# Local attention: the exp of each head taken by ScalarE from PSUM, with the negated maximum as bias and the total as accumulator output

## What is computed

```
sim  = einsum('bhwie,bhwje->bhwij', bq, bk2) * QK_SCALE
sim  = where(mask, -max, sim)
attn = softmax(sim, -1)
out  = einsum('bhwij,bhwje->bhwie', attn, bv2)
```

## Time and profile before

| | us |
|---|---|
| median of 3 runs | 4217.94 |
| lowest and highest | 4217.25, 4219.12 |
| the profiled execution | 4230.46 |
| its span, first to last instruction | 4228.0 |

### The profile page before, as it was taken

How to read it: one execution, slowest core, us unless ns; L and a number is a source line. 1 busy time by engine, 2 the same in 40 slices (tenths; PEclk the granted TensorE clock), 3 DMA queues, 4 the chain that set the end, 5 groups by cost and what they waited for, 6 DMA issues and landing times. The chain is left out here.

```text
span 4228.0 us, 154817 instructions
## 1 busy us (share of the span) xinstructions
PE 3986.5 (94%) x61339; PEld 2359.9 (56%) x61339; DVE 3368.7 (80%) x5724; ACT 2583.2 (61%) x5027; POOL 2537.1 (60%) x2772
## 2 busy tenths in 40 slices
PE   5888697999999999999999999999999999999998
PEld 3555486555554555545555545555455555455554
DVE  5777455899976999958999769999489997699994
ACT  4776222566665666665666656666666666566665
POOL 2111133777763777727777537777277775477771
PEclk8999998999999999999999999999999999999999
DMA  2000000000000000000000000000000000000001
GB/s 72 0 0 1 0 0 3 3 0 0 0 21 7 0 0 0 0 21 6 0 0 0 21 6 0 0 0 0 21 6 0 0 0 21 6 0 0 0 0 41
DMA packets 12340, 27.26 MB, mean 6 GB/s; under 512 B 2460, under 2 KB 6728, under 8 KB 11344
## 3 DMA queue, kind: packets, MB, share of 16 engines
q1 hardware_dynamic: 12240, 25.72, 1.7%
HBM read 23.62 MB, written 2.10 MB: 6 GB/s over the span
## 5 line engine op out<-in xcount | busy, mean ns | idle before, releaser
L954 POOL TENSOR_TENSOR w_t<-w_t 128x512 f32<-128x512 f32 x768 | 981.2, 1278 | 509.0 <-DVE w_t L1259 508.8
L1259 DVE TENSOR_TENSOR w_t<-banks,w_tab 128x512 f32<-128x512 f32 x1536 | 981.6, 681 | 46.1 <-PE banks L1130 27.7
L989 POOL TENSOR_TENSOR w_t<-w_t,w_rn 128x512 f32<-128x512 f32 x768 | 784.9, 1043 | 243.1 <-ACT w_rn L1434 243.1
L1069 PE MATMUL banks<-w_vo,w_xs 128*32 128x256 f32 x12288 | 823.2, 385 | 8.6 <-ACT w_us L1382 8.6
L1130 PE MATMUL banks<-w_qk,w_xs 128*128 128x512 f32 x1536 | 767.2, 622 | 5.8 <-issue 4.1
L1069 PEld LDWEIGHTS banks<-w_vo,w_xs 128*32 128x32 f32 x12288 | 321.7, 109 | 499.8 <-issue 368.6
L1393 ACT ACTIVATE w_pr<-w_pr 128x512 f32<-128x512 f32 x384 | 242.0, 630 | 581.8 <-DVE w_pr L1306 581.8
L1382 ACT ACTIVATE w_us<-banks 128x512 f32<-128x512 f32 x768 | 457.3, 596 | 173.1 <-PE banks L1069 173.1
L1288 DVE TENSOR_REDUCE w_ss<-w_sq 128x16 f32<-128x1024 f32 x384 | 464.3, 1209 | 0.0
L1108 PE MATMUL banks<-w_us,w_prT 128*32 128x128 f32 x10752 | 418.3, 276 | 20.7 <-issue 9.4
L981 POOL TENSOR_TENSOR w_pr<-w_pr,w_rl 128x512 f32<-128x512 f32 x384 | 403.1, 1050 | 35.0 <-DVE w_rl L1274 35.0
(11 more groups left out here) (176 smaller groups left out, 5838.2 us busy)
## 6 DMA issues: line engine op xcount, KB each, us to landing
w_qk<-w_qk_in SPq DMA_DIRECT2D x7, 1024.0 KB, 4.8
w_v<-w_v_in SPq DMA_DIRECT2D x7, 512.0 KB, 5.5
w_o<-w_o_in SPq DMA_DIRECT2D x7, 512.0 KB, 6.3
m_w<-m_w_in SPq DMA_DIRECT2D x6, 342.0 KB
xT<-x_in SPq DMA_DIRECT2D x4, 512.0 KB
out<-kept SPq DMA_DIRECT2D x8, 256.0 KB, 2.4
m_w<-m_w_in SPq DMA_DIRECT2D x6, 171.0 KB
r_tab<-r_tab_in SPq DMA_DIRECT2D x1, 512.0 KB
```

The source lines that it names most:

```text
L954: nc.gpsimd.tensor_tensor(v1, v1, v2[:, :, ::-1, :], ALU.add).then_inc(S["added"], 1)
L989: nc.gpsimd.tensor_tensor(v1, v1, rn[j % 2][:, i * HALF:(i + 1) * HALF].unsqueeze(2) .broadcast_to([P, HALF, WD]), ALU.mult).then_inc(S["n ...
L1069: last = nc.tensor.matmul(banks[WIN * g:WIN * (g + 1), 2, lo:lo + 2 * P], x[:, WIN * w:WIN * (w + 1)], wvo[:, first:first + 2, :].rearrang ...
L1259: nc.vector.tensor_tensor(dst[j % 2][:, i * C:(i + 1) * C].rearrange("p (h d) -> p h d", d=WD), src, tab[:, 2 * t + cs, i * WD:(i + 1) * W ...
```

## The change

VectorE no longer subtracts the maximum and no longer adds up the exps. Its reduction writes the negated maximum (`negate=True`). ScalarE reads the masked scores of each head (2 windows x 32 keys) from PSUM, with that head's negated maximum as per-partition bias, and writes exp to `w_pr`; the sum over the 64 keys goes to the head's column of `w_tot` as accumulator output. This makes 8 ACTIVATEs of 64 elements out of one of 512. The semaphores `w_centred` and `w_totalled` go, and `w_exped` counts 8 a step. TensorE's scores wait for it where they waited for `w_centred`. ScalarE waits for the maximum, and for the turned probabilities of the step that used the same buffer of `w_pr`, a wait that VectorE had before.

```diff
@@ TensorE
-                            pe.wait_ge(S["centred"], passed(n(2) * 2))
+                            pe.wait_ge(S["exped"], passed(n(2) * HALF))
@@ VectorE
-                        dve.wait_ge(S["exped"], passed(n(2)))
-                        nc.vector.tensor_reduce(tot[j2 % 2][:], pr[j2 % 2][:].rearrange("p a h r -> p h a r"),
-                                                mybir.AxisListType.XY, ALU.add).then_inc(S["totalled"], 1)
-                        dve.wait_ge(S["totalled"], passed(n(2)))
+                        dve.wait_ge(S["exped"], passed(n(2) * HALF))
                         nc.vector.reciprocal(rl[j2 % 2][:], tot[j2 % 2][:]).then_inc(S["inverse"], 1)
...
-                        nc.vector.tensor_reduce(mx[j1 % 2][:], heads, mybir.AxisListType.XY, ALU.max)\
+                        nc.vector.tensor_reduce(mx[j1 % 2][:], heads, mybir.AxisListType.XY, ALU.max, negate=True)\
                             .then_inc(S["maxed"], 1)
-                        dve.wait_ge(S["maxed"], passed(n(1)))
-                        if live(3):
-                            dve.wait_ge(S["p_turned"], passed(n(3)))
-                        for par in range(2):
-                            nc.vector.tensor_tensor(
-                                pr[j1 % 2][:, :, par * NPAIR:(par + 1) * NPAIR].rearrange("p a g r -> p g a r"),
-                                heads[:, par], mx[j1 % 2][:, par * NPAIR:(par + 1) * NPAIR].unsqueeze(2).unsqueeze(3)
-                                .broadcast_to([P, NPAIR, 2, WIN]), ALU.subtract).then_inc(S["centred"], 1)
@@ ScalarE
-                        act.wait_ge(S["centred"], passed(n(2) * 2))
-                        p = pr[j2 % 2][:].rearrange("p a h r -> p (a h r)")
-                        nc.scalar.activation(p, p, ACT.Exp).then_inc(S["exped"], 1)
+                        act.wait_ge(S["maxed"], passed(n(2)))
+                        if live(4):
+                            act.wait_ge(S["p_turned"], passed(n(4)))
+                        heads = banks[:, 5:7, 0:2 * P].rearrange("p b (a g r) -> p b g a r", a=2, r=WIN)
+                        for head in range(HALF):
+                            nc.scalar.activation(pr[j2 % 2][:, :, head], heads[:, head // NPAIR, head % NPAIR], ACT.Exp,
+                                                 bias=mx[j2 % 2][:, head:head + 1],
+                                                 accum_out=tot[j2 % 2][:, head:head + 1]).then_inc(S["exped"], 1)
```

More of the change, by code:

```diff
@@ L61 @@
 w_logged w_rnorm w_added w_normed w_turned w_q_turned w_k_turned w_u_made w_u_taken w_edged w_scored w_masked w_maxed
-w_centred w_exped w_totalled w_inverse w_weighted w_p_turned w_p_taken w_valued w_y_taken w_y_turned w_residual
+w_exped w_inverse w_weighted w_p_turned w_p_taken w_valued w_y_taken w_y_turned w_residual
 w_ready w_tabled
@@ L858, in layers @@
         "weights mlp_weights shifted0 shifted1 fused fused_taken0 fused_taken1 qk q_squared k_squared k_rotated q_rotated sums "
-        "guarded logged rnorm added normed turned q_turned k_turned u_made u_taken edged scored masked maxed centred "
-        "exped totalled inverse weighted p_turned p_taken valued y_taken y_turned residual ready tabled").split()}
+        "guarded logged rnorm added normed turned q_turned k_turned u_made u_taken edged scored masked maxed "
+        "exped inverse weighted p_turned p_taken valued y_taken y_turned residual ready tabled").split()}
     M = {n: sem("m_" + n) for n in (
@@ L1156, in iteration @@
                         centre(1, 1)
-                        pe.wait_ge(S["centred"], passed((layer + 1) * N * 2))
+                        pe.wait_ge(S["exped"], passed((layer + 1) * N * HALF))
                         up(0, 0, 1, True)
```

## The result

The changed kernel takes 4443.02 us (median, 4442.11 to 4444.14) against 4218.53 us before (the median of four executions), a ratio of 1.053 with a 95% interval of 1.0512 to 1.0549: 224.5 us slower, where 290 were forecast. Its profiled execution has a span of 4441.2 us and a mean granted TensorE clock of 0.985, against 0.983 before.

A forecast was written before the change was run, and what follows sets the result against it. TensorE's own work was taken to fill each attention step. A delay of 0.78 us behind ScalarE's exps in 372 steps adds 290 us to 4230.5, giving 4520.5; less 12.5 to the median of runs, 4508 us, range 4215 to 4900.

The forecast's parts named there:

- What bounds the kernel: Attention steps: TensorE's own work fills each step, other engines fit under it; VectorE's relief of about 1.4 us is worth nothing.
- The place of the wait: TensorE's second L1069 waits for ScalarE's copy of the first values, near 0.7 us in nearly every step.
- The accumulator's price: ScalarE: each accumulator output assumed a small operation in the same queue, adding 0.11 us per exp.
- The lower bound of 0.20: ScalarE: 0.203 us from one 64-element exp to the next, pointer included, accumulator not, from the L474 row.
- The term 8c: ScalarE: eight exps a step times the interval from one exp to the next, 0.313 us, giving 2.50 us.
- the prediction's own formula: Delay of TensorE's second L1069 per step: eight exp intervals minus 1.72 us, when positive; forecast 0.78 us in 372 steps.
- The slack: ScalarE's values copy could end only 0.23 us later, or 0.12 in the other kind of step, before TensorE stands.
- Hidden accumulator: Rival on ScalarE: accumulator output costs nothing extra, exp interval about 0.20 us, time stays at 4218 us; chance 0.12.
- Waited-out reads: Rival on ScalarE: each accumulator read waits its exp out, delay 1.81 us a step, 4891 us; chance 0.18.
- The falling clock: Rival: TensorE's stalls also lower its granted clock, 113 us on top of the forecast, 4621 us; chance 0.05.
- Faster: Rival: VectorE's gain reaches TensorE at the turned probabilities, 0.09 us in 186 steps, 17 us, 4201 us; chance 0.04.
- The stop at L1082: TensorE's turned probabilities start 0.09 us late in every second step, just behind the end of GpSimd's weighting.

The follow-up runs named there:

- the last experiment: The kernel before with GpSimd's weighting of the probabilities put ahead of its addition for k: 4318.1 us, ratio 1.0207.

## Why the prediction was right, and where its sizes were off

**What bounds the kernel: right.** TensorE's step was full, and the engine that lost half a millisecond had held nobody up: 0.9999 without the total, 1.049 for 1.053 with the load given back, and VectorE waiting for TensorE's scores in both kernels.

**The place of the wait: right.** The second L1069 for the values copy, 372 times; nothing at L1082 or L1174. Removing exactly this copy from behind the exps removed most of the loss.

**The accumulator's price: a little too high.** I took 0.11 us on top of 0.203; the reads add 0.09 and the interval is 0.293 rather than 0.313. The lower bound of 0.20 came out in the kernel without accumulators. That the read would be a small operation of its own was assumed, not read from a row; it came true. The term 8c was 2.50 and measured 2.33 to 2.34. That is the term that was mis-sized: with c = 0.293 the prediction's own formula gives 8 x 0.293 - 1.72 = 0.62 us a step and 372 x 0.62 = 231 us, against the 224.5 measured.

**The other terms of the sum: near.** First exp at +0.48, +0.56, +0.64 and +0.29 in the four kinds of step, 0.49 in the mean for 0.475. Square q to the end of the copy: 1.60 us (1253.53 to 1255.13) for 1.66. The slack was counted up to 0.25 us too small for work put behind the old exp, which only the one added copy brought out: the prediction has ScalarE's rows overlap everywhere, and between exp and square q they didn't. In the forecast it hardly mattered, because 0.475 + 8c measures from the maximum and not from the old exp; what remains of it is the 0.06 us of 1.60 for 1.66. L1069 is late by 0.52, 0.70, 0.67 and 0.43 in the four kinds, 0.58 in the mean for a forecast 0.78; mean length of a step 8.19 for 7.61. Not in the forecast at all is the delay at L1108 in one step of four, some 9 us, which the kernel without accumulators shows alone. What releases L1108 there stays open.

**The rivals.** Hidden accumulator: no, the read is an instruction of its own. Waited-out reads (c = 0.44): no, a read starts 0.20 us after its exp and the next exp 0.09 after the read. The falling clock: no, 0.985 granted against 0.983, though TensorE stands for 8% of the attention. Faster: VectorE's relief brought nothing. The stop at L1082 is in fact gone in the changed kernel (1.00 us behind L1069 in all four kinds of step, where two had 1.07 and 1.09), but only because L1069 itself comes later.

**What the prediction said would show.** The copy ending near 2.1 + 8c = 4.44, with c as measured: it ends at +4.42 in the step shown and at +4.44 in the mean of the four. The wait near 0.7 us in nearly every step: 0.54 in every one. Step length near 8.4: 8.19. VectorE 550 us less busy: 508.

## What to carry to other kernels

Look at what stands behind an operation in its engine's queue, not at the engine's share: here 0.5 us more on ScalarE in each step cost 11 us in all and the next 0.5 us 178, because one copy behind it frees the bank that TensorE wants next. Before moving work off an engine, find one wait on that engine in the critical engine's rows; if there is none, as here, expect nothing from the relief and a price only at the new place. And count an accumulator output as one more instruction for each head: here one reduction of the whole tile on VectorE, which had the time, was cheaper (4239.5 against 4443.0 us).

## What the runs showed of the hardware

- An accumulator output is a second instruction, 0.19 to 0.24 us long, that pushes the next ACTIVATE back by 0.09 us. Exps of 128x64 from PSUM come every 0.20 us without it and every 0.29 with it; from SBUF and without the pointer, every 0.24 with it. The Trainium skill (ScalarE: Activation LUTs, What ACT_TABLE_LOAD costs) gives 280 ns and 0.833 ns per element for an ACTIVATE with pointer bias, and about 93 ns of overlap. An estimate from these figures is 333 ns at 64 elements and 240 ns from one to the next: the duration agrees with the 325 ns in the groups below, the spacing of 0.20 without the accumulator is shorter than that.
- In a full queue ScalarE's instructions come closer together, and their durations don't tell it. The copies and squares of a step come 0.48 us apart behind the exps of the changed kernel, behind the added copies and behind the exps from SBUF, where they were 0.50 or more apart. They last 0.63 to 0.67 us in the first of these, 0.57 to 0.62 in the other two, 0.60 before. Why they are recorded longer behind exps with a pointer stays open. A sum of durations overstates the engine's load; starts are the safer reading here too.
- A VectorE TENSOR_SCALAR of 16 elements on SBUF that started while a GpSimd addition ran ended 0.02 to 0.04 us behind that addition in the cases looked at; it took up to 1.28 us so, and 0.17 where it started as the addition ended. The Trainium skill (SBUF — State Buffer, Who interferes with whom) has tensor_scalar among the operations that can take the port pair shared with GpSimd as an exclusive lock; the rows of the last experiment agree. This hold was harmless until GpSimd's order changed; without the total of the exps it took up all that VectorE had been relieved of.

The groups of instructions by form, ScalarE in the changed kernel (busy us, mean ns | idle before):

```profile
L1385 ACT ACTIVATE w_pr<-banks,w_mx 128x64 f32<-128x64 f32 x3072 | 918.0, 325 | 293.5 <-DVE w_mx L1297 287.2
L1385 ACT ACTIVATION_READ_ACCUMULATOR w_pr<-banks,w_mx 128x1 f32 x3072 | 667.9, 217 | 0.0
```
